# Max aggregation of a graph layer: which edge blocks are gathered and which are built by one-hot products, where the neighbour sums stand, and how the expert weights are fed

## The chip, the cores and the metric

The kernel runs on one core of a Trainium2 chip (trn2), as one launch. The metric is the time of one execution in device microseconds (us). The engines are named as in the profile: PE is TensorE, DVE is VectorE, ACT is ScalarE, POOL is GpSimd and SP is SyncE; PEld is PE's weight load. SP, ACT and POOL each issue DMAs into a queue of their own, and all queues are served by the core's 16 DMA engines.

## The reference

A graph transformer of two layers over N = 625 nodes of width 256 with E = 20,625 edges, sorted by destination. The second half of layer 0 and all of layer 1 matter here:

```python
x = x + L0_ffn(layernorm(x))                 # 8 experts, top 2 of each node
xn = layernorm(x)
msg = (xn @ W_bases)[src]                    # 128 numbers for each edge
agg_sym = segment_sum(msg * sym_w, dst)      # dense products with the adjacency matrix
agg_sum = segment_sum(msg, dst)
agg_max = segment_max(msg, dst)              # the largest of each node's incoming messages
h = einsum(weightings, [agg_sym, agg_sum, agg_max])
x = x + relu(graphnorm(h)) + lambda_attention(xn)
x = x + L1_ffn(layernorm(x))                 # 64 experts of 256 x 512 x 256, top 2 of each node
```

All numbers are float32. The 64 experts' weights alone are 67 MB.

## The kernel before, in words

**Tiling.** The nodes are 5 tiles (NT) of 125 (TP). The edges are 41 blocks (NMB) of 512 (MB); the last, block 40, has 145. Each engine has one program, written in order; semaphores join them. Nothing reorders instructions: what stands first on an engine or a queue goes first.

**End of layer 0.** POOL's `fetch(fys)` (L674) gathers each node's two expert rows into `ya` and `yb`, ten indirect DMAs of 125 rows. DVE's `add_results(0)` (L2168) adds them to `x`. SP issues the first two pairs of layer 1's expert weights (four DMAs of 1 MB, L585 and L586) before that. At the same time PE counts the edges of each node (L1170, 50 small matmuls), and DVE works out from them where each node's edges end (L2198 to L2207); on DVE that stands ahead of `add_results`.

**Bases and sums.** Then come the layer norm, the products with `W_bases` and `W_comb` (L1193, L1198), a store of the bases to DRAM as `btab` (ACT, L1570), a split of the bases into three bfloat16 parts (DVE, L2226 to L2232), and the neighbour sums: for each node tile 5 products of 125 x 256 with the adjacency matrix on PE (L1206) and two copies on DVE (L2240, L2242).

**The loop for the maximum.** For each block of edges the messages, 128 x 512, are brought into PSUM in one of two ways. An even block is built by 15 bfloat16 matmuls (3 parts x 5 node tiles, L1271) from a one-hot matrix, which DVE made for two such blocks at a time by comparing source numbers with node numbers (L2189, five instructions). An odd block is fetched by POOL from `btab` with four indirect DMAs of 128 rows (L729) and transposed by PE (four matmuls, L1277). There are four buffers for fetched blocks, and POOL waits for a buffer until PE has transposed the block that lay in it. DVE then runs a segmented running maximum over the block (L2389); PE transposes the result (L1287), ACT copies it out of PSUM, SP stores it to `rtab`. PE's order is: messages of block b, then the transposed runs of block b-2. The attention of the layer is strewn into the loop by block number: on PE queries (L819, after block 3), keys (L819), values (L1231), transposes (L1240), lambda (L1248), result (L1258); on DVE their counterparts, and from block 23 on the eight `weigh` steps of the sums (L1640, two instructions of 125 x 1280 each). After the loop POOL fetches each node's last run (L736), and DVE weighs the maxima.

**Layer 1's experts.** 32 steps of two experts each (64 node slots for each expert). Step s needs its rows, gathered by POOL (L670, four buffers), and its weights `W1` (1 MB, on SP's queue, L628) and `W2` (1 MB, on POOL's queue, L751). The weights lie in a ring of five pairs of SBUF regions (`EW_AT`, `RING`). Two pairs are loaded early, three more when the weighted sums are done (`c_out` 17, L620), the rest as steps free their regions: `W1` of step s when the hidden products of step s-5 are done, `W2` when the result products of step s-5 are done. PE's step is: transposed hidden rows of s-1 (L1391), transposed rows of s+1 (L1371), hidden products (L1382), result of s-1 (L1405). ACT stores each step's 128 result rows to `ys`.

**The end.** POOL waits for all stores, fetches two rows for each node (`ya` for five tiles, then `yb` for five), DVE adds all of `ya`, then all of `yb`, tests whether an expert was overfull, and SP stores the output as one DMA of 625 KB (L636).

## Time and profile before

| | us |
|---|---|
| median of 3 runs | 991.87 |
| lowest and highest run | 987.62, 994.85 |
| profiled execution | 991.11 |
| its span, first to last instruction | 989.4 |

The profile is of one execution. Its page gives busy time by engine; the chain of waits follows the work that ended last back from the end; the groups by line give the mean duration of each kind of instruction and what ended the idle time before it; the timeline gives instructions in order of time; the table by stretches gives busy time, granted TensorE clock and DMA load between two moments. Times in the rows are us from the start of the span. A busy PE is not PE at its peak, since ends of matmuls are modelled.

| part of the span | from, to (us) |
|---|---|
| layer 0's rows fetched and added | 478.8 to 507.2 |
| layer norm, bases, split, neighbour sums | 507.2 to 542.9 |
| loop for the maximum, to the last running maximum | 547.6 to 702.9 |
| last runs, weighing, graph norm, routing of layer 1 | 702.9 to 778.1 |
| 32 expert steps | 778.1 to 957.2 |
| fetch of results, output | 957.2 to 989.4 |

### The profile page before, as it was taken

What the parts mean: (1) busy time and instruction counts of PE and PEld (TensorE: products, weight loads), DVE (VectorE), ACT (ScalarE), POOL (GpSimd) and SP (SyncE); (2) the same over time, 40 slices, a digit from 0 to 9 for tenths busy, and PEclk for the clock granted to TensorE, in tenths of its full rate; (3) what the DMA queues carried; (4) which work ended last, traced back from release to release, by engine and by line L of the source; (5) the groups of instructions that cost most, each with busy time, mean ns of one, the idle gap of its engine ahead of it and who ended that gap; (6) DMA issues with size and microseconds to landing.
All of it is one profiled execution on the core that took longest, in us unless ns stands there. A gap on an engine that the chain in (4) does not pass through costs nothing.

```text
span 989.4 us, 13447 instructions
## 1 busy us (share of the span) xinstructions
PE 711.3 (72%) x4912; PEld 522.4 (53%) x4912; DVE 485.5 (49%) x1173; ACT 161.1 (16%) x355; POOL 198.0 (20%) x213
## 2 busy tenths in 40 slices
PE   2467767989979619999747789787333597878880
PEld 1355646877868519999545456444212244444440
DVE  7537888656663451111343265588686522222231
ACT  0311311224201104233000021111100011111110
POOL 3000000000000011231503545372200332232213
PEclk9978977899989759999658999898855699999995
DMA  3440100000000066998631355465251499999922
GB/s 110 91 135 1 50 1 1 1 2 1 2 1 2 9 203 215 326 321 277 181 109 37 98 135 155 110 181 141 82 219 62 128 381 410 410 410 410 410 84 72
DMA packets 84500, 147.75 MB, mean 149 GB/s; under 512 B 10961, under 2 KB 57641, under 8 KB 84428
## 3 DMA queue, kind: packets, MB, share of 16 engines
q1 hardware_dynamic: 58438, 84.97, 25.5%
q0 software_dynamic: 18336, 55.09, 16.5%
q10 hardware_dynamic: 7654, 6.75, 2.0%
q8 instruction: 43, 0.70, 0.3%
q14 instruction: 29, 0.24, 0.1%
HBM read 127.45 MB, written 19.31 MB: 148 GB/s over the span
## 4 chain that ended last, share of the span: by engine, by line
PE 48%; DVE 21%; DMA 14%; issue 4%; POOL 3%; ACT 1%; DVEq 1%; POOLq 0%; SPq 0%; ACTq 0%
DMA big<-xn_rows,spots 11%; PE ps L1271 6%; PE ps L1127 5%; PE ps L1141 5%; PE ps L932 5%; DVE arena L1640 4%; PE ps L819 3%; PE ps L978 3%; PE ps L1382 3%; PE ps L1405 2%; DVE arena L2389 2%; PE ps L943 2%; PE ps L918 2%; DVE big L1916 2%; DVE ya L1640 2%
## 5 line engine op out<-in xcount | busy, mean ns | idle before, releaser
L670 POOL DMA_INDIRECT big<-xn_rows,spots x46 | 45.1, 981 | 432.4 <-DVE spots L2047 409.1
L978 PE MATMUL ps<-big 125*128 125x144 bf16 x825 | 94.7, 242 | 19.8 <-DVE big L1640 11.6
L1640 DVE TENSOR_TENSOR arena<-arena,ps 125x400 f32 x110 | 57.9, 526 | 90.4 <-PE ps L980 80.2
L978 PEld LDWEIGHTS ps<-big 125*128 125x128 bf16 x825 | 84.5, 107 | 25.8 <-DVE big L1640 14.4
L1271 PE MATMUL ps<-arena,early 125*128 125x512 bf16 (+1 forms) x315 | 77.2, 402 | 21.7 <-DVE arena L2389 16.3
L980 PE MATMUL ps<-big 125*128 125x64 bf16 x825 | 92.6, 205 | 0.0
L980 PEld LDWEIGHTS ps<-big 125*128 125x128 bf16 x825 | 81.9, 104 | 6.7 <-issue 4.3
L1640 DVE TENSOR_TENSOR big<-ps,b1cols 128x512 f32<-128x512 f32 x32 | 22.1, 691 | 116.9 <-PE ps L1391 116.9
L2389 DVE TENSOR_TENSOR_SCAN arena<-arena,ps 128x512 f32<-128x512 bf16 (+1 forms) x41 | 51.6, 1257 | 47.5 <-PE ps L1287 36.1
L1271 PEld LDWEIGHTS ps<-arena,early 125*128 125x128 bf16 x315 | 31.1, 104 | 62.6 <-DVE arena L2389 19.6
L1382 PE MATMUL ps<-arena,big 128*64 128x512 f32 x256 | 63.7, 619 | 0.0
L1405 PE MATMUL ps<-arena,big 128*64 128x256 f32 x512 | 60.7, 379 | 1.3 <-issue 1.3
L1916 DVE TENSOR_SCALAR big<-iota,srcf 125x640 bf16<-125x640 f16 x165 | 57.9, 380 | 0.0
L932 PE MATMUL ps<-arena,xn 125*128 125x250 f32 (+1 forms) x240 | 51.0, 362 | 8.0 <-ACT tmpf L1476 6.7
L1127 PE MATMUL ps<-big,arena 128*128 128x128 f32 x448 | 54.3, 281 | 2.3 <-DVE big L2137 2.3
L1127 PEld LDWEIGHTS ps<-big,arena 128*128 128x128 f32 x448 | 53.9, 198 | 3.5 <-issue 2.9
L1405 PEld LDWEIGHTS ps<-arena,big 128*64 128x64 f32 x512 | 36.9, 137 | 32.8 <-issue 19.1
L729 POOL DMA_INDIRECT lwo<-btab,srcs x40 | 39.6, 990 | 67.2 <-issue 47.7
L1485 ACT COPY picks<-big 125x624 bf16<-125x624 bf16 x55 | 37.9, 707 | 84.6 <-DVE big L1640 84.2
L1141 PE MATMUL ps<-arena,big 128*128 128x256 f32 x224 | 50.7, 380 | 0.0
L932 PEld LDWEIGHTS ps<-arena,xn 125*128 125x128 f32 x240 | 41.3, 200 | 14.0 <-ACT tmpf L1476 8.1
L729 POOL DMA_INDIRECT kphi<-btab,srcs x40 | 41.2, 1030 | 34.3 <-PE ps L1277 23.6
(356 smaller groups left out, 1108.0 us busy)
## 6 DMA issues: line engine op xcount, KB each, us to landing
arena<-in_L_ffn_W_dram SPq DMA_DIRECT2D x53, 1024.0 KB, 10.2
arena<-in_L_ffn_W_dram POOLq DMA_DIRECT2D x39, 1024.0 KB, 16.5
rtab<-arena SPq DMA_DIRECT2D x40, 256.0 KB, 3.9
arena<-new_node SPq DMA_DIRECT2D x40, 128.0 KB, 3.3
ys<-big ACTq DMA_DIRECT2D x32, 128.0 KB, 7.3
arena<-src_list SPq DMA_DIRECT2D x20, 125.0 KB
arena<-in_L_mix_W_dram SPq DMA_DIRECT2D x2, 1024.0 KB, 6.9
fys<-big ACTq DMA_DIRECT2D x14, 128.0 KB, 3.1
```

Of the source, the lines that this page charges most:

```text
L729: pool.indirect_dma_start(fetched[i % 2][:, 4 * h + j, :], None, btab.ap(), bass.IndirectOffsetOnAxis(ap=srcs[:, c:c + 1].bitcast(U32), ax ...
L932: m = pe.matmul(ps[:, 6, 0:(t1 - t0) * TP], xn[:, s, c * 128:(c + 1) * 128], adj5[:, b, s, t0 * TP:t1 * TP], start=(s == 0), stop=(s == NT ...
L978: pe.matmul(psflat[:, at:at + K2 * WIN], ohs[:, s, u, t * TP:t * TP + 128], pieces[:, 0:K2 * WIN], start=first and t % 2 == 0, stop=False, ...
L980: m = pe.matmul(psflat[:, at + K1 * WIN:at + K2 * WIN], ohs[:, s, u, t * TP:t * TP + 128], pieces[:, K2 * WIN:KC * WIN], start=False, stop ...
L1127: m = pe.matmul(ps[:, 2 + 2 * (c % 2) + h, m_ * 128:(m_ + 1) * 128], fw1[:, c % 2, k, (4 * h + m_) * 128:(4 * h + m_ + 1) * 128], fxT[:, c ...
L1141: m = pe.matmul(ps[:, 6 + c % 2, 0:D], fh[:, c % 2, k, :], fw2[:, c % 2, k, :], start=(k == 0), stop=(k == 7))
L1271: m = pe.matmul(ps[:, 6 + b % 2, 0:n], split[:, t, k, :], onehot[:, i % 2, t, h * MB:h * MB + n], start=(k == 0 and t == 0), stop=(k == 2 ...
L1382: m = pe.matmul(ps[64 * e:64 * e + 64, 2 + s % 2, :], xeT[:, s % 2, k, 64 * e:64 * e + 64], ew[s % RING][0][:, e, k * H1:(k + 1) * H1], st ...
L1405: m = pe.matmul(ps[64 * e:64 * e + 64, 6 + s % 2, 0:D], hact[:, s % 2, k, 64 * e:64 * e + 64], ew[s % RING][1][:, e, k * D:(k + 1) * D], s ...
L1640: return v.tensor_tensor(out, p, q, op)
L1916: return v.tensor_scalar(ohs[:, s, u, :], iota16[0:EP, :], col, None, ALU.is_equal)
L2389: v.tensor_tensor_scan(runs[:, b % 2, 0:n], arep[:, b % 4, 0:n], ps[:, 6 + b % 2, 0:n], runs[:, (b - 1) % 2, MB - 1:MB] if b else -3e38, A ...
```

## The change

1. **Blocks.** Every third block (0, 3, ..., 39) and block 40 are built by one-hot products, 15 in all; the other 26 are fetched. Before it was 21 and 20. POOL issues 104 gathers in the loop in place of 80; DVE makes 8 one-hot sets in place of 11. There are still four buffers for fetched blocks.
2. **Neighbour sums.** They move into the loop: tiles 0 and 1 after block 0, tiles 2, 3, 4 after blocks 1, 2, 3, on PE and on DVE. The queries move from block 3 to 4 on PE and from 4 to 5 on DVE. PE tests for unsorted edges once in place of twice.
3. **`btab`** is stored by node tiles, five DMAs on ACT's queue.
4. **Weights behind the fetch.** SP waits for both halves of the fetch of layer 0's rows before it issues the first two pairs of expert weights.
5. **Ring of seven.** Two more pairs of regions, made of memory that is free by then (bias rows, the mixing weights, turned rows, old keys); buffers are merged so that they are contiguous. Five pairs are issued at `c_out` 17, but for the last `W2`, which waits for the routing (`spots_out` 2). The store of the normalised rows moves from SP to ACT.
6. **Results by tiles.** The last fetch goes tile by tile (`ya`, `yb` of tile 0, then tile 1, ...), DVE adds tile by tile, and SP stores each tile (125 KB) when it is added, without waiting for DVE's test.
7. Some semaphores are shared, to make room for others (`types_ready`, `comp_ready` and `row_ready` become counts of `edges_ready`); what waits for what is the same.

On PE, between the products with `W_bases` (L1193, now L1210) and the test that opens the loop. Before:

```order
L1193 MATMUL ps<-wbc,xnT 125x224 x10
L1198 MATMUL ps<-xnT,wbc 128x313 x4
L1206 MATMUL ps<-yb,arena 125x256 x25
L1291 TENSOR_LOAD loose
L1291 ISA x2
L1292 COMPARE_AND_BRANCH
```

And of the change, on PE at the same place:

```order
L1210 MATMUL ps<-wbc,xnT 125x224 x10
L1215 MATMUL ps<-xnT,wbc 128x313 x4
L1307 TENSOR_LOAD loose
L1307 ISA x2
L1309 COMPARE_AND_BRANCH
```

The 25 products of the neighbour sums (`yb,arena`) have left the place ahead of the test.

On PE, the first blocks of the loop. `arena,early` (now `arena,kept`) are the one-hot products, `ident,lwo` and `ident,kphi` (now `mixw`, `kept`) the transposes of a fetched block, `ident,arena` those of the runs. Before:

```order
L1271 MATMUL ps<-arena,early 128x512 x15
L1277 MATMUL ps<-ident,lwo 128x128 x4
L1271 MATMUL ps<-arena,early 128x512 x15
L1287 MATMUL ps<-ident,arena 128x128 x4
L1277 MATMUL ps<-ident,lwo 128x128 x4
L1287 MATMUL ps<-ident,arena 128x128 x4
L819 MATMUL ps<-xnT,wq 128x313 x8
```

And of the change, on PE, blocks 0 to 3:

```order
L1286 MATMUL ps<-arena,kept 128x512 x15
L1221 MATMUL ps<-yb,arena 125x256 x10
L1293 MATMUL ps<-ident,mixw 128x128 x4
L1221 MATMUL ps<-yb,arena 125x256 x5
L1293 MATMUL ps<-ident,mixw 128x128 x4
L1303 MATMUL ps<-ident,arena 128x128 x4
L1221 MATMUL ps<-yb,arena 125x256 x5
L1286 MATMUL ps<-arena,kept 128x512 x15
L1303 MATMUL ps<-ident,arena 128x128 x4
L1221 MATMUL ps<-yb,arena 125x256 x5
```

Two fetched blocks now stand in a row between one-hot blocks, and each of the first four blocks is followed by neighbour sums.

On POOL, the start of the expert steps: `big<-xn_rows,spots` is a gather of rows, `arena<-in_L_ffn_W_dram` the load of a `W2`. Before:

```order
L670 DMA big<-xn_rows,spots 128x256 [waits spots_out,xn_stored]
L670 DMA big<-xn_rows,spots 128x256 x3
L670 DMA big<-xn_rows,spots 128x256 [waits s_xT] x2
L751 DMA arena<-in_L_ffn_W_dram 128x2x1024 [waits s_y]
L670 DMA big<-xn_rows,spots 128x256 [waits s_xT]
L751 DMA arena<-in_L_ffn_W_dram 128x2x1024 [waits s_y]
```

And of the change, on POOL at the same place:

```order
L685 DMA big<-xn_rows,spots 128x256 [waits spots_out,xn_stored]
L685 DMA big<-xn_rows,spots 128x256 x3
L685 DMA big<-xn_rows,spots 128x256 [waits s_xT] x4
L764 DMA arena<-in_L_ffn_W_dram 128x2x1024 [waits s_y]
L685 DMA big<-xn_rows,spots 128x256 [waits s_xT]
L764 DMA arena<-in_L_ffn_W_dram 128x2x1024 [waits s_y]
```

The first `W2` that POOL loads stands behind two more gathers, and is that of step 7 in place of step 5.

The core of the diff:

```diff
-NSET = -(-NMB // 4)
-NGOT = NMB // 4
+SPREAD = [b for b in range(NMB) if b % 3 == 0 or b == NMB - 1]
+GOT = [b for b in range(NMB) if b not in SPREAD]
+NSET = -(-len(SPREAD) // 2)
...
-        RING = len(EW_AT)
+        ew.append([rows[:, 0:8, :].rearrange("p (e a) d -> p e (a d)", e=2),
+                   mixw[:, 0:2048].rearrange("p (e n) -> p e n", e=2)])
+        ew.append([turned2[:, 0:2048].rearrange("p (e n) -> p e n", e=2),
+                   kept2[:, 0:2048].rearrange("p (e n) -> p e n", e=2)])
+        RING = len(ew)
...
+            for k in range(2):
+                sp.wait_ge(y_got[k], 80)
             for s in range(2):
                 sp.dma_start(ew[s][0], w1v[s]).then_inc(ew1_loaded[s], 16)
                 sp.dma_start(ew[s][1], w2v[s]).then_inc(ew2_loaded[s], 16)
...
             sp.wait_ge(c_out, 17)
             for s in range(2, RING):
                 sp.dma_start(ew[s][0], w1v[s]).then_inc(ew1_loaded[s], 16)
-                sp.dma_start(ew[s][1], w2v[s]).then_inc(ew2_loaded[s], 16)
-            sp.wait_ge(norm_ready, 6)
-            sp.dma_start(node_major(xn_rows[1].ap()), xn[:, :, :]).then_inc(xn_stored, 16)
+                if s < RING - 1:
+                    sp.dma_start(ew[s][1], w2v[s]).then_inc(ew2_loaded[s], 16)
+            sp.wait_ge(xn_stored, 32)
+            sp.wait_ge(spots_out, 2)
+            sp.dma_start(ew[RING - 1][1], w2v[RING - 1]).then_inc(ew2_loaded[RING - 1], 16)
             for s in range(RING, E1 // 2):
                 sp.wait_ge(s_h, s - RING + 1)
                 sp.dma_start(ew[s % RING][0], w1v[s]).then_inc(ew1_loaded[s % RING], 16)
...
+                for t in range(NT):
+                    sp.wait_ge(sparse_done, t + 1)
+                    sp.dma_start(a["out"][t * TP:(t + 1) * TP, :], x[:, t, :]).then_inc(o_stored, 16)
+                sp.wait_ge(o_stored, 16 * NT)
...
-                for i in range(NGOT):
-                    for h in range(2):
-                        if i >= 2:
-                            pool.wait_ge(msg_mm, 4 * (i - 2) + 2 * h + 2)
-                        for j in range(4):
-                            c = 4 * (4 * i + 2 * h + 1) + j
-                            pool.indirect_dma_start(fetched[i % 2][:, 4 * h + j, :], None, btab.ap(),
...
+                for q, b in enumerate(GOT):
+                    if q >= 4:
+                        pool.wait_ge(msg_mm, GOT[q - 4] + 1)
+                    for j in range(4):
+                        c = 4 * b + j
+                        pool.indirect_dma_start(fetched[q // 2 % 2][:, 4 * (q % 2) + j, :], None, btab.ap(),
...
-            fetch(ys)
+            for t in range(NT):
+                for k in range(2):
+                    pool.indirect_dma_start((ya, yb)[k][:, t, :], None, ys.ap(),
...
-            pe.wait_ge(c_out, 7)
-            for t in range(NT):
-                if t >= 2:
-                    pe.wait_ge(c_out, 7 + t - 1)
+            def neighbour_sums(t):
+                pe.wait_ge(c_out, 7 if t < 2 else 7 + t - 1)
                 for s in range(NT):
                     m = pe.matmul(ps[0:TP, t % 2, 0:2 * DB], adjT[:, s, t * TP:(t + 1) * TP], bas[:, s, :],
                                   start=(s == 0), stop=(s == NT - 1))
                 cproduct(m)
-            pe.wait_ge(c_out, 12)
...
-                    if b == 3:
+                    if b == 0:
+                        neighbour_sums(0)
+                        neighbour_sums(1)
+                    if 1 <= b < NT - 1:
+                        neighbour_sums(b + 1)
+                    if b == 4:
                         attend_queries()
...
-            act.wait_ge(c_out, 5)
-            act.dma_start(node_major(btab.ap()), bas[:, :, 0:DB]).then_inc(btab_stored, 16)
+            for t in range(NT):
+                act.wait_ge(c_out, t + 1)
+                act.dma_start(btab.ap()[t * TP:(t + 1) * TP, :], bas[:, t, 0:DB]).then_inc(btab_stored, 16)
...
-            add_results(1).then_inc(sparse_done, 1)
-            dve.wait_ge(sparse_done, 1)
+            for t in range(NT):
+                dve.wait_ge(y_tile[t][0], y_tile[t][1] + 32)
+                done(v.scalar_tensor_tensor(out=x[:, t, :], in0=ya[:, t, :], scalar=gate[:, t, 2:3], in1=x[:, t, :],
+                                            op0=ALU.mult, op1=ALU.add))
+                v.scalar_tensor_tensor(out=x[:, t, :], in0=yb[:, t, :], scalar=gate[:, t, 3:4], in1=x[:, t, :],
+                                       op0=ALU.mult, op1=ALU.add).then_inc(sparse_done, 1)
+            dve.wait_ge(sparse_done, NT)
```

## Rows read from the trace of the kernel before

**Rows 1.** By stretches: us; busy PE, PEld, DVE, ACT, POOL; granted clock, DMA share, GB/s.

```profile
547.50:595.30 47.80, 42.56 (x201) 26.20 (x202) 23.44 (x33) 7.69 (x14) 22.26 (x24) 0.93 0.46 116
595.30:640.50 45.20, 37.91 (x194) 24.51 (x193) 26.96 (x46) 7.71 (x14) 19.73 (x21) 0.92 0.52 142
640.50:703.00 62.50, 49.09 (x267) 27.60 (x266) 54.17 (x56) 11.80 (x21) 26.75 (x24) 0.92 0.53 147
```

**Rows 2.** Timeline, end of layer 0: start, us, engine, instruction, idle before it.

```profile
487.86 10.66 PE L1170 MATMUL ps<-ones,arena 125*125 125x1 f32 x50 [0.51 <-DVE x L1640]
...
505.10 2.07 DVE L2173 SCALAR_TENSOR_TENSOR x<-yb,gate,x 125x256 f32<-125x256 f32 x5 [0.57 <-DMA yb<-fys,get]
```

**Rows 3.** Chain of waits, the fetch: start, us, what.

```profile
493.21 11.79 DMA yb<-fys,get
```

**Rows 4.** Timeline, from the bases to the first gather of the loop.

```profile
521.82 2.27 PE L1198 MATMUL ps<-xnT,wbc 128*128 128x313 f32 x8
...
527.02 0.82 DVE L1640 TENSOR_TENSOR early<-big,early 125x640 bf16<-125x640 f32 x1
...
529.00 13.25 PE L1206 MATMUL ps<-yb,arena 125*125 125x256 f32 x50 [4.91 <-DVE yb L2233]
531.78 0.96 POOL L729 DMA_INDIRECT lwo<-btab,srcs  x1 [37.37 <-issue]
```

**Rows 5.** Timeline of PE in the loop.

```profile
547.58 4.85 PE L1271 MATMUL ps<-arena,early 125*128 125x512 bf16 x15 [5.32 <-issue]
...
665.70 3.41 PE L1271 MATMUL ps<-arena,early 125*128 125x512 bf16 x15 [0.70 <-DVE arena L2389]
...
673.08 5.10 PE L1271 MATMUL ps<-arena,early 125*128 125x512 bf16 x15 [2.65 <-DVE arena L2389]
678.01 0.60 PE L1287 MATMUL ps<-ident,arena 128*128 128x128 f32 x4
```

**Rows 6.** Timeline of DVE in the loop: a one-hot set, a weigh step, block 40.

```profile
665.56 2.05 DVE L2189 TENSOR_SCALAR arena<-arena,nodeid 125x1024 bf16<-125x1024 f16 x5
...
670.22 1.49 DVE L1640 TENSOR_TENSOR ya<-ya,arena 125x1280 f32<-125x1280 f32 x1
...
702.41 0.52 DVE L2389 TENSOR_TENSOR_SCAN arena<-arena,ps 128x145 f32<-128x145 bf16 x1 [0.41 <-PE ps L1287]
```

**Rows 7.** Groups of POOL from 531 to 640: count, busy us, mean ns, idle before.

```profile
L729 POOL DMA_INDIRECT lwo<-btab,srcs x32 | 30.5, 954 | 64.7 <-issue 45.3 <-PE ps L1277 19.4
```

**Rows 8.** Groups of POOL from 640 to 680.

```profile
L729 POOL DMA_INDIRECT kphi<-btab,srcs x16 | 18.0, 1125 | 17.4 <-PE ps L1277 13.1 <-issue 4.3
```

**Rows 9.** Timeline of POOL, the slowest gather.

```profile
668.89 2.11 POOL L729 DMA_INDIRECT kphi<-btab,srcs  x1 [0.30 <-issue]
```

**Rows 10.** The gathers of the loop (L729) by themselves.

```profile
DMA to landing us min/median/max: 2.4/3.4/8.3
```

**Rows 11.** Table by stretches, as rows 1: ahead of the expert steps, and in them.

```profile
730.00:780.00 50.00, 15.43 (x62) 11.60 (x64) 35.29 (x115) 2.12 (x4) 4.73 (x5) 0.53 0.36 139
...
800.00:940.00 140.00, 116.12 (x737) 61.07 (x734) 36.80 (x72) 23.58 (x50) 40.27 (x47) 1.00 1.03 411
```

**Rows 12.** Timeline, first refills of the ring, SP's and POOL's.

```profile
782.88 26.77 SPq L628 DMA_DIRECT2D arena<-in_L_ffn_W_dram  x7
...
788.41 0.75 POOL L751 DMA_DIRECT2D arena<-in_L_ffn_W_dram  x1 [6.87 <-PE ps L1405]
```

**Rows 13.** Chain of waits, a step that waits for its rows, and the end.

```profile
918.35 17.43 DMA big<-xn_rows,spots
...
974.07 4.11 DMA yb<-ys,get
978.27 2.08 DVE x L2173 x5
```

**Rows 14.** Timeline, the output.

```profile
981.68 0.35 SPq L636 DMA_DIRECT2D out_dram<-x  x1
```

**Rows 15.** The stores of the steps' rows (L1615) by themselves.

```profile
DMA to landing us min/median/max: 1.7/7.3/9.4
```

More of the change, by code:

```diff
@@ L1291, in _ @@
             slow = pe.value_load(loose[0:1, 0:1], min_val=0, max_val=E)
+            products = nc_[0]
             with pe.If(slow > 0):
+                for t in range(NT):
+                    neighbour_sums(t)
                 attend_queries()
@@ L1328, in _ @@
             with pe.Else():
+                nc_[0] = products
                 pe.wait_ge(split_ready, 1)
@@ L2236, in _, with neighbour_sums @@
             m.then_inc(c_out, 1)
-            for t in range(NT):
+            def neighbour_sums(t):
                 dve.wait_ge(c_mm, 7 + t)
@@ L2335, in _ @@
             with dve.If(slow > 0):
+                for t in range(NT):
+                    neighbour_sums(t)
+                dve.wait_ge(c_out, 12)
                 weigh(0, 8)
@@ L2368, in _ @@
                 dve.wait_ge(mx_turned, 1)
-                for t in range(NT - 2):
-                    mark_free(v.memset(held[:, :], 0.0))
                 mark_free(v.tensor_copy(agg[:, 0:4, 2 * DB:3 * DB],
```

135 lines of the change are left out of this document (73 added, 62 removed).

## The prediction

> **What bounds the kernel now.** I read the chain of waits first, then the stretches, then the timeline of each engine around the six edits. Three stretches matter.
>
> The loop for the maximum runs from PE's first one-hot product at 547.58 [rows 5] to DVE's last running maximum at 702.41 + 0.52 = 702.93 [rows 6], 155.4 us. No single engine fills it. In its first part (blocks 0 to 9) PE is busy 42.6 of 47.8 us, in the second (10 to 20) 37.9 of 45.2, in the third (21 to 40) DVE 54.2 of 62.5 [rows 1]. POOL is busy less than half of each. The rest is PE and DVE waiting for one another.
>
> The expert steps are held by DMA: from 800 to 940 its share is 1.03 at 411 GB/s [rows 11], and a step waits for its rows, which land 17.43 after their issue behind the weights [rows 13]. Ahead of the steps, from 730 to 780, DMA is busy only 0.36.
>
> The fetch at the end of layer 0 looks like a third: its last gather takes 11.79 to land [rows 3], beside 4 MB of weights, against 4.11 for the same gather in the end [rows 13]. But DVE's addition of `yb` had idled only 0.57 for it [rows 2].
>
> **The change, part by part.**
>
> *Weights behind the fetch.* Without the weights the last gather lands about 493.2 + 4.1 = 497.3, eight earlier. PE's 50 counting products (487.86 to 498.52 [rows 2]) and what DVE makes of them stand ahead of the additions, and are not touched. So only the 0.57 goes; from then on the counts are what is late. The weights move behind the fetch, about 497 to 508, where they hide under the layer norm; the loop's lists are ahead of them on SP's queue. Term: **-0.6**, carried into the loop's start.
>
> *Neighbour sums and the test.* PE is free of the bases at 521.82 + 2.27 = 524.1; the split is ready at 527.84 [rows 4]. The two tests ahead of the loop cost 5.32 of idle PE [rows 5]; one costs between half of that and all, so PE is through between 526.8 and 529.4. I take 528.4, the middle and later than the split, less the 0.6: the first one-hot product at **527.8** in place of 547.58.
>
> *`btab` by tiles, start of the gathers.* The first gather is at 531.78 [rows 4]. Five stores in place of one may end a microsecond earlier or later; I take nothing but the 0.6: **531.2**.
>
> *The loop, by PE and DVE.* A one-hot block costs PE 3.41, or 5.10 after an idle time of 2.65; a fetched one 0.60 [rows 5], so each exchange saves PE 2.8. First part: PE's 42.6, plus the sums' 13.25 [rows 4], less 2.8 for one exchange (five one-hot blocks become four) is 53.0; at the higher clock the sums are some 2 shorter, waits are 0 to 2: I take 52. Second part: 37.9 less three exchanges is 29.5, plus the 7.3 that PE idles now is 36.8; since block 21's one-hot now stands behind the attention's result I take 38. Third part: DVE's 54.2 less one set of one-hots (2.05 [rows 6]) is 52.1, and of its 8.3 idle, which were mostly waits for one-hot blocks, I keep 3: 55. Together 145, so the last maximum would be at 527.8 + 145 = 672.8.
>
> *The loop, by POOL.* It now has 26 blocks of four gathers. A gather takes 0.954 + 0.30 [rows 7, 9] while DVE is little used, 1.125 + 0.30 beside the weigh steps [rows 8, 9]. With 72 of the first and 32 of the second kind, 90.3 + 45.6, the last is issued by 667.1 if the four buffers never hold POOL up, and lands 3.4 later [rows 10], at 670.5. Block 38 is the last fetched; after it come its transposes, two one-hot blocks (one short), their turns and maxima, about 7.5 by rows 5 and 6: 678. That is the later of the two sums and they are close, so each will now and then wait for the other: I take **679**. Term: 702.9 - 679 = **-24**. Ends: 670 if they interleave without loss (-33), 690 below. The early move of the queries by a block and the shared semaphores cost nothing: PE does the work of block 4 meanwhile, and the counts rise in the old order.
>
> *Ring of seven.* Four megabyte DMAs leave the saturated stretch: 4.19 MB at 411 GB/s is 10.2 us. They go to the stretch from 730, where 139 of some 410 GB/s are used [rows 11]; five pairs are there by about 23 us after their issue, before the steps begin. Against it: POOL's first `W2` stands behind two more gathers, each freed by a turned block, and comes about 1.7 later than now (788.41 [rows 12]), which at half the bandwidth is 0.9; and `W1` (released from 782.88 on) can run further ahead of rows and `W2` than now, which leaves PE more steps to do after the last byte. For that I take 1.3. Term: **-8**; ends -14 (DMA and PE end together) and 0. The last `W2` goes out beside the first rows and may hold up the first step: **+0.5** (0 to 1.5). The rows' store on ACT's queue is hidden by the routing, which lasts to 774.
>
> *Results by tiles.* The ten gathers end as now. DVE then has two of ten instructions left, 0.83 in place of 2.08 [rows 13], and SP needn't wait for DVE's test: it issues at about 979.1 in place of 981.68 [rows 14], 2.6 earlier. From there to the span's end (989.4) 7.7 pass now for 625 KB. For 125 KB the store may take as little as 1.7 [rows 15], or, if the time is all fixed, 7.7; I take 4.8. Term: **-5.5**; ends -2.6 and -8.6.
>
> A page of the Trainium skill speaks against that term. "DMA: Bandwidth & Descriptors", section "Anatomy of one DMA", gives a DMA about 2.0 us plus its bytes at 436 GB/s; by it the shorter store would save only 1.2 and the term would be -3.8. The 7.7 above holds more than it states, so the trace does not settle it.
>
> **Sum.** -24 - 8 + 0.5 - 5.5 = -37. The profiled execution took 991.1, so 954.1; the median of the runs is 0.8 above it, so **955**.
>
> **The rivals.**
>
> *The gathers set the pace throughout.* POOL's idle times for a free buffer go, and DVE is denser than now, so all 104 may take 1.425: 148.2. Then the last maximum is at 531.2 + 148.2 + 3.4 + 7.5 = 690.3 and the loop gives 12.6: 966. For it: rows 8 against rows 7. Against it: in the first two parts DVE has no weigh steps. Chance 0.2.
>
> *All overlaps work.* PE and DVE interleave (-33), the ring gives 12, the end 8: -52.5, so 939. For it: PE's 13 us of sums fall into waits for the first gathers. Against it: the three engines hand over for each block. Chance 0.14.
>
> *The ring gives nothing.* Steps wait for rows, not for weights [rows 13]; if the rows queue longer behind more weights, PE ends where it does now: 963. Against it: DMA is saturated, and it has 10 us less to move. Chance 0.08.
>
> *DVE shuts POOL out.* If POOL waited out each of DVE's one-hot sets (six in the loop, 2.05 each) and weigh steps (sixteen of about 1.49 [rows 6]), 36 us, the gathers would need 104 x 1.254 + 36 = 166.4, the loop would end at 708.5, 5.6 later than now: 984. Rows 8 show 0.17 a gather beside such work, not a whole instruction, and one of 2.11 [rows 9]. Chance 0.05.
>
> The Trainium skill, "SBUF — State Buffer", section "Who interferes with whom", states such a rule: VectorE in a two-port mode holds the port pair that GpSimd needs to write descriptors for the whole instruction. By it the gathers would be about as in the last paragraph; the trace shows the effect, at a tenth of that size.
>
> *Slower: gathers crowd each other out.* 26 blocks' gathers run beside the same stores and lists in a shorter loop. Each gather would have to take over 1.67 for the kernel to lose what ring and end give (531.2 + 104 x 1.67 + 10.9 = 715.8, which is +13), and 1.77 for 1% more. At 1.9 the loop ends at 739.7: 1016. For it: the 2.11 + 0.30 of the slowest gather [rows 9]. Against it: DMA's share in the loop is about half [rows 1]. Chance 0.03.
>
> **How the numbers follow.** The forecast, 948 to 962, has 0.5. Below 940 lies about half of the second rival (0.07), above 970 the last two (0.08); so 940 to 970 holds a little over 8 in 10. About 1%, some 10 us, is what a measurement of this kernel can tell from no change, its three runs being 7 apart. Faster by more than that: all cases but the last two, 0.92; within it: the shut-out POOL, 0.05; slower: 0.03.
>
> **What would show it.** The addition of `yb` waits for nothing, and DVE's count is what precedes it. The first one-hot product stands near 528 and the neighbour sums lie among the first blocks. POOL waits for few buffers, and its gathers step by 1.25, later 1.4; the last maximum is near 679. Seven pairs are loaded by 775 on the old clock, and DMA is saturated some 10 us less. The last output store is issued within a microsecond of the last addition. It is wrong if the gathers step by over 1.5, if the loop takes more than 160 us from its first product, or if the steps' total stays at 179 us.

## The result, and the profile after

The changed kernel takes **954.31 us** (median of 4 runs, 950.98 to 958.77) against 991.38 for the kernel before beside it: a ratio of **0.963**, 95% interval 0.958 to 0.968. Forecast were 955 in a range of 940 to 970. The time fits; not all of its terms do, and one stretch of the profiled execution owes nothing to the change.

The profiled execution took 950.98, the fastest of the four; its span is 949.3 against 989.4. The stretches of the loop, cut as in [rows 1] (us; busy PE, PEld, DVE, ACT, POOL; granted clock, DMA share, GB/s):

```profile
521.70:575.70 54.00, 47.95 (x229) 33.25 (x230) 25.59 (x43) 7.64 (x14) 38.40 (x41) 0.94 0.45 119
575.70:614.90 39.20, 33.54 (x186) 23.60 (x184) 24.91 (x41) 7.81 (x14) 29.93 (x31) 0.96 0.66 176
614.90:676.00 61.10, 44.29 (x233) 24.89 (x232) 52.52 (x51) 11.57 (x20) 36.32 (x33) 0.86 0.57 156
```

They took 54.0, 39.2 and 61.1 us; forecast were 52, 38 and 55. POOL is now busy for two thirds of the loop. The third stretch is where the forecast is off: the granted clock is 0.86 there, and DVE, busy 52.5 of 61.1, waits for one-hot products.

The timeline (start, us, engine, line, instruction, number, and in brackets the idle time before it and what ended it). L1187 are PE's counting products, L2199 the additions of layer 0's rows, L1286 the one-hot products, L743 the gathers, L2416 the running maximum, L1404 the first hidden product of a step, L651 the output:

```profile
474.59 0.70 PE L1079 MATMUL ps<-ident,picks 125*8 125x125 f32 x5 [1.67 <-issue]
...
480.90 10.66 PE L1187 MATMUL ps<-ones,arena 125*125 125x1 f32 x50 [0.51 <-DVE x L1666]
...
497.97 2.07 DVE L2199 SCALAR_TENSOR_TENSOR x<-yb,gate,x 125x256 f32<-125x256 f32 x5
...
515.63 2.27 PE L1215 MATMUL ps<-xnT,wbc 128*128 128x313 f32 x8
...
521.70 4.99 PE L1286 MATMUL ps<-arena,kept 125*128 125x512 bf16 x15 [3.81 <-DVE kept L1666]
...
525.06 0.96 POOL L743 DMA_INDIRECT mixw<-btab,srcs  x1 [32.70 <-issue]
...
626.70 5.10 PE L1286 MATMUL ps<-arena,kept 125*128 125x512 bf16 x15 [2.28 <-DVE arena L2416]
...
638.00 4.87 PE L1286 MATMUL ps<-arena,kept 125*128 125x512 bf16 x15 [3.14 <-DVE arena L2416]
...
659.20 6.20 PE L1286 MATMUL ps<-arena,kept 125*128 125x512 bf16 x15 [3.13 <-DVE arena L2416]
...
675.40 0.52 DVE L2416 TENSOR_TENSOR_SCAN arena<-arena,ps 128x145 f32<-128x145 bf16 x1 [0.41 <-PE ps L1303]
...
752.54 3.68 PE L1404 MATMUL ps<-arena,big 128*64 128x512 f32 x8 [0.25 <-DVE big L2503]
...
756.26 9.99 SPq L640 DMA_DIRECT2D arena<-in_L_ffn_W_dram  x3
...
765.20 0.77 POOL L764 DMA_DIRECT2D arena<-in_L_ffn_W_dram  x1
...
933.99 12.56 SPq L651 DMA_DIRECT2D out_dram<-x  x5
...
945.77 0.48 DVE L2526 SCALAR_TENSOR_TENSOR x<-yb,gate,x 125x256 f32<-125x256 f32 x1
```

Against [rows 2]: `yb` is added with no wait, where it had waited 0.57. Against [rows 4, 5]: the first one-hot product stands at 521.70, 6.1 behind the start of L1215; before, 25.8 lay between the same two. Against [rows 6]: the last maximum ends at 675.92. Against [rows 12]: the refills begin at 756.26 (SP) and 765.20 (POOL), 3.7 and 12.7 behind the first hidden product, where they had come 3.7 and 9.2 behind it. Against [rows 14]: the last output store is issued at 946.3, right behind the last addition (945.77 + 0.48), and the span ends 3.0 later; from the store to the end it had been 7.7.

The gathers by themselves (for [rows 7 to 10]), with what they waited for and who waited for them:

```profile
L743 POOL DMA_INDIRECT mixw<-btab,srcs x56: 940/947/1718, 525.1 to 660.2; - x56
...
  PE ps L1293: 1.0, 3
...
  PE ps L1293: 2.9, 2
...
DMA to landing us min/median/max: 2.4/3.5/6.7
```

POOL makes 104 gathers (these 56 and 48 into the other buffer, `kept`) from 525.06 to 661.16, one each 1.309 us; buffers held it up for 1.0 us in all, and PE waited for gathered rows for 2.9. Four waits of the expert steps remain in the chain of waits, for [rows 13]:

```profile
800.36 20.94 DMA big<-xn_rows,spots
822.12 23.90 DMA big<-xn_rows,spots
846.85 24.06 DMA big<-xn_rows,spots
871.74 22.09 DMA big<-xn_rows,spots
```

The chain of the kernel before has six such waits, of 16.3 to 19.2; now there are four, of 21 to 24.

### The profile page after: what moved, and what is told of

The parts are those of the page before. It is cut to its first block, busy times and chain, and to the rows that moved or that the text cites. A ratio compares the mean times of both kernels' runs of the same rounds, so it can differ in the third digit from the quotient of the medians.

```text
span 949.3 us, 13321 instructions
## 1 busy us (share of the span) xinstructions
PE 692.8 (73%) x4846; PEld 514.7 (54%) x4846; DVE 480.1 (51%) x1158; ACT 161.2 (17%) x355; POOL 220.8 (23%) x235
## 4 chain that ended last, share of the span: by engine, by line
PE 51%; DVE 21%; DMA 13%; issue 3%; POOL 2%; ACT 1%; DVEq 1%; POOLq 0%; ACTq 0%; SPq 0%
DMA big<-xn_rows,spots 11%; PE ps L1144 6%; PE ps L1158 5%; PE ps L949 5%; PE ps L1286 4%; DVE arena L1666 4%; PE ps L836 4%; PE ps L1404 3%; PE ps L995 3%; PE ps L1427 3%; DVE arena L2416 2%; PE ps L960 2%; PE ps L935 2%; DVE big L1942 2%; DVE ya L1666 2%
## 5 line engine op out<-in xcount | busy, mean ns | idle before, releaser
L995 PE MATMUL ps<-big 125*128 125x144 bf16 x825 | 94.3, 241 | 19.2 <-DVE big L1666 11.5
L1286 PE MATMUL ps<-arena,kept 125*128 125x512 bf16 (+1 forms) x225 | 57.9, 418 | 19.9 <-DVE arena L2416 16.1
L2416 DVE TENSOR_TENSOR_SCAN arena<-arena,ps 128x512 f32<-128x512 bf16 (+1 forms) x41 | 51.5, 1257 | 39.3 <-PE ps L1303 32.9
L743 POOL DMA_INDIRECT mixw<-btab,srcs x56 | 55.8, 997 | 49.5 <-issue 49.2
L743 POOL DMA_INDIRECT kept<-btab,srcs x48 | 48.8, 1018 | 14.7 <-issue 14.0
L1286 PEld LDWEIGHTS ps<-arena,kept 125*128 125x128 bf16 x225 | 22.8, 108 | 51.5 <-DVE arena L2416 18.7
L1404 PE MATMUL ps<-arena,big 128*64 128x512 f32 x192 | 50.4, 648 | 0.2 <-DVE big L2503 0.2
L1427 PE MATMUL ps<-arena,big 128*64 128x256 f32 x384 | 46.2, 383 | 1.3 <-issue 1.3
L1158 PEld LDWEIGHTS ps<-arena,big 128*128 128x128 f32 x224 | 41.5, 190 | 5.1
## 6 DMA issues: line engine op xcount, KB each, us to landing
turned<-in_L_ffn_W_dram SPq DMA_DIRECT2D x4, 1024.0 KB, 16.6
```

Source lines behind the costliest of these rows:

```text
L743: pool.indirect_dma_start(fetched[q // 2 % 2][:, 4 * (q % 2) + j, :], None, btab.ap(), bass.IndirectOffsetOnAxis(ap=srcs[:, c:c + 1].bitca ...
L995: pe.matmul(psflat[:, at:at + K2 * WIN], ohs[:, s, u, t * TP:t * TP + 128], pieces[:, 0:K2 * WIN], start=first and t % 2 == 0, stop=False, ...
L1158: m = pe.matmul(ps[:, 6 + c % 2, 0:D], fh[:, c % 2, k, :], fw2[:, c % 2, k, :], start=(k == 0), stop=(k == 7))
L1286: m = pe.matmul(ps[:, 6 + b % 2, 0:n], split[:, t, k, :], onehot[:, i % 2, t, h * MB:h * MB + n], start=(k == 0 and t == 0), stop=(k == 2 ...
L1404: m = pe.matmul(ps[64 * e:64 * e + 64, 2 + s % 2, :], xeT[:, s % 2, k, 64 * e:64 * e + 64], ew[s % RING][0][:, e, k * H1:(k + 1) * H1], st ...
L1427: m = pe.matmul(ps[64 * e:64 * e + 64, 6 + s % 2, 0:D], hact[:, s % 2, k, 64 * e:64 * e + 64], ew[s % RING][1][:, e, k * D:(k + 1) * D], s ...
```

## The experiments

Each is the changed kernel with the edit shown (the last three with several), timed beside the kernel before on the same chip, which took 989.1 to 989.6 us each time. "The control" is the first of them, and +x us is the difference of the medians to it. The stretches below are from one profile each; the medians judge.

### The changed kernel again

> The changed kernel itself, unaltered, as the yardstick for the others of this call. Both theories: 954 us, ratio 0.963 to the kernel before (0.958 to 0.968). Its one profile is looked at for the idle time of TensorE ahead of the counting products of layer 0, which was 5.69 us in the kernel before and 1.67 us in the changed one: if that gap belongs to the changed program, it is again 1.5 to 2 us; if it varies from execution to execution, it may be 5 to 6.

955.21 us (949.23 to 957.81), ratio 0.964 (0.961 to 0.968). Its profile, of 955.88, shows ahead of layer 0's expert bias:

```profile
479.32 1.20 PE L1079 MATMUL ps<-ident,picks 125*8 125x125 f32 x5 [5.92 <-issue]
```

The same program that idled 1.67 there now idles 5.92. Among 14 profiles (before, after, and the twelve here) the gap is 1.67 or 1.68 in three and 4.89 to 6.50 in eleven, the kernel before among these. The counting products stand at 486.66 here, so 5.8 of the 7.0 us that those of the profile above are earlier (487.86 to 480.90) are of that execution, not of the change; 4.25 of them are this gap. This second profile is the fairer partner of the one before:

| stretch, us | before | changed (c0) | difference | forecast |
|---|---|---|---|---|
| start to the counting products | 487.9 | 486.7 | -1.2 | 0 |
| to the first one-hot product | 59.7 | 39.7 | -20.0 | -19.8 |
| the loop, to the last maximum | 155.4 | 154.5 | -0.9 | -4.1 |
| to the first hidden product | 76.3 | 77.3 | +1.1 | |
| the expert steps | 178.0 | 171.3 | -6.7 | -7.5 |
| behind the last result product | 32.3 | 24.7 | -7.5 | -5.5 |
| span | 989.4 | 954.2 | -35.2 | -37 |

The table says when things happen, not which edit pays for it: the neighbour sums left the second row and entered the third. That is what the undoing is for.

### Weights ahead of the fetch again

```diff
-            for k in range(2):
-                sp.wait_ge(y_got[k], 80)
             for s in range(2):
                 sp.dma_start(ew[s][0], w1v[s])...
```

> The first four loads of expert weights of layer 1 (two W1, two W2) go out at once again, ahead of the fetch of layer 0's rows, as in the kernel before; all else is the changed kernel. Theory (the fetch had been late for DVE by 0.57 us only, so nearly all of it was hidden): 955 us, 0.5 to 0.7 us more than the changed kernel, and DVE waits 0.4 to 0.7 us ahead of its add of the yb rows. Rival (the loads also held up TensorE, and the 4 us that its counting products start earlier after the change come from here): 958 to 960 us, and in its profile TensorE idles 5 to 6 us ahead of the counting products.

957.48 us (956.84 to 959.67), ratio 0.967 (0.964 to 0.971): 2.3 above the control, with overlapping intervals. Its addition of `yb`:

```profile
504.89 2.07 DVE L2197 SCALAR_TENSOR_TENSOR x<-yb,gate,x 125x256 f32<-125x256 f32 x5 [1.15 <-DMA yb<-fys,get]
```

A wait of 1.15 in place of none, and PE's gap is 6.16, no longer than the control's 5.92. The order of the weights is worth one to two microseconds, a little more than the theory's 0.7; the rival's 4 us aren't from it.

### Ring of five

```diff
+        ew = ew[:5]
         RING = len(ew)
...
-                if s < RING - 1:
-                    sp.dma_start(ew[s][1], w2v[s]).then_inc(ew2_loaded[s], 16)
-            sp.wait_ge(xn_stored, 32)
-            sp.wait_ge(spots_out, 2)
-            sp.dma_start(ew[RING - 1][1], w2v[RING - 1]).then_inc(ew2_loaded[RING - 1], 16)
+                sp.dma_start(ew[s][1], w2v[s]).then_inc(ew2_loaded[s], 16)
```

> Ring of five weight sets in place of seven, with all nine or ten halves loaded as the kernel before did (both halves of sets 2 to 4 behind the sum over the nodes); all else is the changed kernel. Theory (the stretch of the expert steps is paced by weight bytes once the ring is used up, and two more sets were worth 6.2 us of it net, forecast 7.5): 960 to 962 us, the stretch from the first hidden product to the last result product 177 to 179 us in place of 171.7. Rival (two sets more give nothing, the 6 us are from elsewhere): 953 to 955 us and 171 to 173.

963.72 us (957.81 to 964.84), ratio 0.972 (0.969 to 0.976): +8.5. The expert steps take 179.9 from the first hidden to the last result product (756.96 to 936.81), against 171.3 in the control; the loop takes 153.9 (154.5 there). The rival falls; the ring is worth a little more than the theory's 6.2.

### One output store

```diff
-                for t in range(NT):
-                    sp.wait_ge(sparse_done, t + 1)
-                    sp.dma_start(a["out"][t * TP:(t + 1) * TP, :], x[:, t, :]).then_inc(o_stored, 16)
-                sp.wait_ge(o_stored, 16 * NT)
+                sp.wait_ge(sparse_done, NT)
+                sp.dma_start(node_major(a["out"]), x[:, :, :]).then_inc(o_stored, 16)
+                sp.wait_ge(o_stored, 16)
```

> The result is stored by one transfer behind the last tile's sum, as in the kernel before, not by five tile by tile; the fetch and the sums stay tile by tile. Theory (from the last sum to the end of the span it took 9.0 us before, 3.1 us after; the store was worth most of the end's 7.2 us): 958 to 960 us, and 7.5 to 9 us from the last sum to the end of the span. Rival (the five stores hide no more than one does, and the gain at the end came from sums made while rows were still being fetched): 954 to 955 us.

960.84 us (958.31 to 965.08), ratio 0.971 (0.967 to 0.974): +5.6. In the timeline:

```profile
953.08 0.48 DVE L2525 SCALAR_TENSOR_TENSOR x<-yb,gate,x 125x256 f32<-125x256 f32 x1
953.59 0.35 SPq L650 DMA_DIRECT2D out_dram<-x  x1
```

From the issue of the whole store to the end of the span (961.9) pass 8.3 us; from that of the last fifth 3.0. That is the gain of the end but for about 2 us: two additions stand behind the last rows in place of five, and SP no longer waits for DVE's test (in the kernel before the store was issued 1.3 us behind the last addition, here at once).

### Sums ahead of the loop

```diff
                 nc_[0] = products
+                for t in range(NT):
+                    neighbour_sums(t)
                 pe.wait_ge(split_ready, 1)
...
-                    if b == 0:
-                        neighbour_sums(0)
-                        neighbour_sums(1)
-                    if 1 <= b < NT - 1:
-                        neighbour_sums(b + 1)
```

(and the same on DVE)

> The neighbour sums are made ahead of the loop on TensorE and VectorE again, as in the kernel before, but with the loop's one test; all else is the changed kernel. Theory (inside the loop they cost TensorE 11.4 us of products in a first stretch where it is busy for 48 of 54 us, so moving them in gave only a part of the 13 to 14 us that they take ahead of it): 959 us (957 to 963), first one-hot product 13 to 14 us later, loop 5 to 11 us shorter. Rival (inside the loop they fill time in which TensorE waits and cost nothing): 967 to 969 us and a loop as long as the changed kernel's 154.

955.21 us (953.41 to 956.36), ratio 0.965 (0.964 to 0.967): the control's time to the last digit. Neither theory gave zero. PE of this kernel, then of the control, from the sums (L1221) to the queries' products (L836):

```profile
528.75 13.39 PE L1221 MATMUL ps<-yb,arena 125*125 125x256 f32 x50 [4.91 <-DVE yb L2256]
541.98 3.40 PE L1286 MATMUL ps<-arena,kept 125*128 125x512 bf16 x15
...
552.68 4.38 PE L836 MATMUL ps<-xnT,mixw 128*128 128x313 f32 x16
```

```profile
526.40 6.25 PE L1286 MATMUL ps<-arena,kept 125*128 125x512 bf16 x15 [3.81 <-DVE kept L1666]
532.48 4.48 PE L1221 MATMUL ps<-yb,arena 125*125 125x256 f32 x20
...
550.96 4.45 PE L836 MATMUL ps<-xnT,mixw 128*128 128x313 f32 x16
```

With the sums ahead, the first one-hot product is 15.6 later, but the queries come 1.7 later only, and L1215 had begun 1.3 later already. PE is busy nearly without a gap in either order, so moving its own work does nothing: what came off ahead of the loop was put into it. Even the wait for the split (3.81, now ahead of the one-hot product) has its twin (4.91, ahead of the sums), and the first one-hot product takes 3.40 behind 13.4 us of products, but 6.25 behind an idle time. From L1215 to the first one-hot product it is 20.4 here and was 25.8 in the kernel before: the **tests** give about 5.3. The branches of PE's sequencer (PEldq; ns, then when they begin), of the kernel before and, below, of the changed one:

```profile
L1292 PEldq COMPARE_BRANCH  x1: 339/339/339, 543.5 to 543.5; - x1
L1302 PEldq COMPARE_BRANCH  x1: 2840/2840/2840, 544.6 to 544.6; - x1
```

```profile
L1309 PEldq COMPARE_BRANCH  x1: 3545/3545/3545, 515.0 to 515.0; - x1
```

The gain is the place of the test, not that there is one less. The branch that is left takes longer than both before, but it stands ahead of a wait of PE and is over at 518.6, when PE still waits for the split until 521.7 (with the sums ahead: 3.28, over at 524.7, while PE waits for the bases until 528.75). In the kernel before both tests stood behind the sums, where PE waited for nothing else. And the loop without the sums takes 140.3 against 155.4 before: the **exchange of blocks** gives some 15.

### Half the blocks by one-hot products, a quarter

```diff
-SPREAD = [b for b in range(NMB) if b % 3 == 0 or b == NMB - 1]
+SPREAD = [b for b in range(NMB) if b % 2 == 0]
```

> Every second edge block by one-hot products (21 of 41 in place of 15), the other 20 by 80 gathers in place of 104, as in the kernel before; sums in the loop, ring and end as changed. Theory (the exchange of blocks pays: six blocks more cost TensorE about 5.0 against 1.2 us each, and VectorE three sets of 2.05 us): loop 164 to 170 us, 965 to 970 us in all. Rival (the loop fell from 155.4 to 154 although the sums went in, so the exchange gave little; something else paces it): 953 to 957 us.

968.97 us (967.44 to 969.53), ratio 0.979 (0.978 to 0.981): +13.8; the loop takes 165.2 (522.61 to 687.80). The exchange pays as expected; POOL, with 80 gathers, waited 34.5 us for buffers.

With `b % 4 == 0`:

> Every fourth edge block by one-hot products (11 of 41), 30 by 120 gathers; all else as changed. Theory (POOL's step of 1.309 us is next behind TensorE: 120 gathers take 157 us from 529.7, the last lands at 689 to 690, the loop ends 9 to 12 us later): 963 to 967 us, and TensorE waits for gathered rows in the last stretch. Rival (TensorE and VectorE set the pace, and four one-hot blocks fewer save them 15 us, half of it on the path): 946 to 950 us.

971.83 us (966.85 to 974.70), ratio 0.981 (0.979 to 0.983): +16.6, more than expected; the loop takes 170.8 (527.68 to 698.46). PE's waits for gathered rows (us in total, times, longest):

```profile
PE ps L1293 <- DMA mixw<-btab,srcs: 18.9, 7, 4.8
PE ps L1293 <- DMA kept<-btab,srcs: 16.2, 5, 5.0
```

35 us of waiting, against 1.4 in the control: here POOL is the bound. Of the three shares tried a third is the best; both neighbours cost 14 to 17 us.

### Four PSUM banks

```diff
-                    pe.wait_ge(run_step, b - 1)
+                    pe.wait_ge(run_step, b - 1 if b < 22 else b - 3)
...
+def bank(b):
+    return 6 + b % 2 if b < 22 else (6, 7, 0, 1)[b % 4]
```

(the blocks' products, transposes and maxima use `bank(b)` in place of `6 + b % 2`)

> From block 22 on the messages of the blocks take four PSUM banks in turn in place of two (the two others are free by then), so that TensorE may begin a block's products one running maximum earlier; all else as changed. Theory (in the last third of the loop VectorE waits some 8 us for one-hot products that could start only when the running maximum two blocks back was done; with the bank free they start while VectorE still weighs): the stretch from 614.9 to 676.0, 61.1 us, takes 54 to 57, 948 to 951 us in all. Rival (the waits belong to VectorE's own work and to the low clock, and move elsewhere): 953 to 956 us.

953.85 us (946.69 to 955.99), ratio 0.962 (0.959 to 0.965): not apart from the control. The timeline of the last third:

```profile
641.26 4.35 PE L1292 MATMUL ps<-arena,kept 125*128 125x512 bf16 x15
...
649.93 1.03 PE L1299 MATMUL ps<-ident,mixw 128*128 128x128 f32 x4 [3.00 <-DMA mixw<-btab,srcs]
...
660.89 1.09 PE L1299 MATMUL ps<-ident,kept 128*128 128x128 f32 x4 [2.64 <-DMA kept<-btab,srcs]
...
672.09 1.08 PE L1299 MATMUL ps<-ident,mixw 128*128 128x128 f32 x4 [4.24 <-DMA mixw<-btab,srcs]
...
673.82 5.13 PE L1292 MATMUL ps<-arena,kept 125*128 125x512 bf16 x15
...
679.60 1.93 DVE L2422 TENSOR_TENSOR_SCAN arena<-arena,ps 128x512 f32<-128x512 bf16 x2 [4.05 <-PE ps L1309]
```

The one-hot products do begin without a wait. In their place PE waits 3.00, 2.64 and 4.24 for gathered rows. The wait was taken away, and POOL, a few us behind, took its place: the stretch fell from 61.8 to 58.8 only. So two bounds of the loop lie near each other here.

### The pattern moved by a block

```diff
-SPREAD = [b for b in range(NMB) if b % 3 == 0 or b == NMB - 1]
+SPREAD = [b for b in range(NMB) if b % 3 == 1 or b == 0]
```

> The same numbers of blocks by one-hot products (15) and by gathers (26), but the pattern moved by one block: one-hot are 0, 1, 4, 7, ... 37, 40 in place of 0, 3, 6, ... 39, 40. All else as changed. Theory (at the loop's start TensorE waits for what the first eight gathers bring, whether the sums stand ahead of the loop or in it, since the gathers start at 530 either way and step by 1.3; and behind the last gather there are two one-hot blocks): the queries' products, at 551 in the changed kernel, stand at 545 to 549; from the last gather's issue to the last maximum it takes 10 to 12 us in place of 15; 948 to 952 us. Rival (TensorE's and VectorE's work alone sets the loop's length, whatever the order of the blocks): 954 to 956 us.

967.25 us (965.77 to 969.90), ratio 0.978 (0.976 to 0.980): **+12**, where both theories had at most +1. My theory of the loop's start falls: the queries stand at 551.72, no earlier. In the timeline, turns of runs (L1303) that wait for ACT:

```profile
574.82 1.09 PE L1303 MATMUL ps<-ident,arena 128*128 128x128 f32 x4 [5.19 <-ACT arena L1607]
...
612.33 1.09 PE L1303 MATMUL ps<-ident,arena 128*128 128x128 f32 x4 [4.44 <-ACT arena L1607]
...
614.92 6.27 PE L1286 MATMUL ps<-arena,kept 125*128 125x512 bf16 x15 [1.50 <-DVE arena L2416]
```

ACT copies a block's turned runs into one of two buffers, which come free when the store to `rtab` has landed (42 us of ACT's waits end with such a store). Here PE idles 5.19 and 4.44 behind such copies (once, 2.43, in the control), and after the second the next one-hot product takes 6.27. In the control ACT waits even longer for stores in all (53 us); what differs is that PE stands behind it twice. By the end of the attention's result this loop is 12.4 behind the control (627.7 against 615.4), 3.4 of it the one-hot block that now stands ahead and 7.2 PE's longer waits for ACT; from there on both need 65.5 or 65.6.

### The same pattern with banks and weigh steps eased

```diff
+WEIGH_AT = (4, 11, 15, 20, 24, 27, 30, 33)
...
-                    if b in range(23, 39, 2):
-                        weigh((b - 23) // 2, (b - 23) // 2 + 1)
+                    if b in WEIGH_AT:
+                        weigh(WEIGH_AT.index(b), WEIGH_AT.index(b) + 1)
```

(with the four banks and the moved pattern; a wait of DVE moves from block 5 to 4 with the first of these steps)

> As the shifted pattern, with four PSUM banks from block 22 on and the eight weigh steps behind blocks 4, 11, 15, 20, 24, 27, 30, 33 in place of 23, 25, ... 37. Theory (with banks alone TensorE waited 12.5 us for gathered rows, and VectorE's work fills the last third; with both eased POOL's 136 us are the bound): the last maximum 5 to 8 us behind the last gather's issue, so at 672 to 675 us against 681; 945 to 949 us. Rival (POOL is not the bound, and VectorE's steps only move): 950 us or more, with TensorE waiting under 3 us for gathered rows.

960.53 us (956.73 to 962.89), ratio 0.970 (0.968 to 0.972): 6.7 better than the moved pattern alone, 5 worse than the control. A miss, and not the rival's case either: PE waited 9.1 us for gathered rows. It waited for ACT once more, 14.6 us in six waits.

With 17 one-hot blocks and 24 gathered:

```diff
+SPREAD = [0, 1, 2, 4, 7, 10, 12, 15, 17, 20, 22, 25, 27, 30, 33, 36, 40]
```

> As the one before, with 17 blocks by one-hot products (0, 1, 2, 4, 7, 10, 12, 15, 17, 20, 22, 25, 27, 30, 33, 36, 40) and 24 by 96 gathers. Theory (POOL was the bound of the one before; eight gathers fewer free 10.5 us of it, and TensorE pays 3 to 5 us a block for two): 942 to 946 us, 3 us below the one before, with TensorE waiting under 4 us for gathered rows. Rival (TensorE is the bound by then): 4 to 8 us above the one before.

964.98 us (962.01 to 966.02), ratio 0.975 (0.973 to 0.977): 4.5 above the one before, the rival's size. PE waited 3.4 us for gathered rows and 13.3 for ACT. Fewer gathers didn't help here. That the loop is now held by its stores is the reading of these waits, not shown by a run: how much of these three runs' loss is the store and how much the order of the attention's steps, wasn't taken apart.

### Pattern of the changed kernel, banks, and the last block gathered

```diff
-SPREAD = [b for b in range(NMB) if b % 3 == 0 or b == NMB - 1]
+SPREAD = [b for b in range(NMB - 2) if b % 3 == 0] + [NMB - 3, NMB - 1]
...
-                    if b in range(23, 39, 2):
-                        weigh((b - 23) // 2, (b - 23) // 2 + 1)
+                    if b == 20 or b in range(23, 37, 2):
+                        weigh((b - 21) // 2 if b > 20 else 0, (b - 21) // 2 + 1 if b > 20 else 1)
```

(with the four banks)

> The pattern of the changed kernel, with four PSUM banks from block 22 on, block 38 by one-hot products and block 39 by gathers (so that only the short block 40 stands behind the last gathered one), and the weigh steps one place earlier (behind blocks 20, 23, 25, ... 35). Theory (with four banks TensorE waited 9.9 us for gathered rows at blocks 32, 35 and 38, and a one-hot product of 5.1 us stood behind the last of them; now it is made while those rows come): from the last gather's issue to the last maximum 7 to 9 us in place of 12.9, 947 to 951 us. Rival (the length of the loop hangs on how one-hot products and VectorE's steps fall on one another, as the pattern moved by one block showed, and any move here costs as much as it gives): 953 to 960 us.

**946.92 us** (943.27 to 951.54), ratio **0.959** (0.956 to 0.961): below both kernels. Its end of the loop:

```profile
660.86 3.40 PE L1292 MATMUL ps<-arena,kept 125*128 125x512 bf16 x15
...
666.13 0.63 PE L1299 MATMUL ps<-ident,mixw 128*128 128x128 f32 x4 [1.43 <-DMA mixw<-btab,srcs]
...
667.40 1.93 DVE L2422 TENSOR_TENSOR_SCAN arena<-arena,ps 128x512 f32<-128x512 bf16 x2 [1.22 <-PE ps L1309]
```

The one-hot product of block 38 is made while the last rows come, and from the issue of the last gather (662.1) to the last maximum (669.33) pass 7.2 us, as the theory had. The loop takes 149.0 against the control's 154.5; these 5.5 are of the three edits together. Its profile, of 943.27, has the short gap (1.68) ahead of the expert bias; the median is over five runs. Its interval just touches the control's, so that it is faster than the changed kernel is likely, not certain.

## Why the prediction was right, and where it wasn't

**Weights behind the fetch** (-0.6). Right: the wait of 0.57 is gone, and 1.15 comes back when the edit is undone. What seemed 7 us in the first profile is 1.2 in the second; no edit stands there.

**First one-hot product** (547.58 to 527.8). Right in size: 19.98 less between counting products and first one-hot product, forecast 19.8 with the fetch's 0.6. Its step for the test was wrong, and luck that this cost little: I let one test, at half of 5.32 or more, run behind the bases' products and end 0.6 behind the split (528.4 is also not the middle of 526.8 and 529.4, which is 528.1). The test ran beside these products and ended 3.1 ahead of the split, and the split alone set the time (the wait of 3.81 for `kept`). And the term isn't a gain for its larger part: the sums' 14 us go into the loop and stay there whole (undone: 0.0). What is left is the tests' 5.3.

**The loop by PE and DVE** (145). This step failed: 154.5. The third stretch was put at 55 and took 61 to 62. I kept 3 of 8.3 us of DVE's waits; it still waits 8.6 (61.1 less 52.5). Four of the products it waits for take 4.87 to 6.20, after idle times of 2.1 to 3.1, and can't start until the maximum two blocks back has left their bank: with four banks they start without a wait. The other two stretches are 2 and 1 longer than forecast. **The loop by POOL** (151, 679) was the later of the two sums and gave the answer: the last maximum is at 680.85. It was right by a bound that doesn't bind. The gathers themselves came as forecast, 136.1 us for 135.9; but from the last one's end to the last maximum 14.8 passed, forecast 10.9, and PE waits only 1.4 to 2.9 us for gathered rows, all at the loop's start. Only when the banks are eased does it (9.9 us), and by then nearly nothing is left to win. Two sums within 6 us of each other made the total safe, not the reasoning; and that the whole is right to 1 us is luck, since the loop gave 3 us less than forecast, the end 2 more and the start 1 more.

**Ring of seven** (-7.5 net). Right: 6.7 by the profiles, 8.5 by undoing it. The bytes left the stretch as forecast: 352 GB/s for 171.3 us in place of 363 for 178.0 are 4.3 MB less, and in the 48 us ahead DMA moves 215 GB/s in place of 140.

**Results by tiles** (-5.5). Too small: 7.5, of which the store is 5.4 to 5.6. I took the middle between 1.7 and 7.7 for the last store to the end of the span; it is 3.0, near the low end, while the whole one takes 8.3 (7.7 in the kernel before). The Trainium skill, "DMA: Bandwidth & Descriptors", section "Anatomy of one DMA", gives its 2.0 us plus bytes at 436 GB/s for DMAs that GpSimd issues, by which the difference would be an estimated 1.2. These stores go out on SP's queue, the runs show 5.3, and they decide.

**The rivals.** Gathers that set the pace throughout would need 1.425 each; they take 1.309. That DVE shuts POOL out falls by its price, not by its kind. The mean of [rows 8] hid that a gather does wait out DVE:

```profile
626.57 1.46 DVE L1666 TENSOR_TENSOR arena<-weights,big 125x1280 f32<-125x1280 f32 x1
...
627.13 1.72 POOL L743 DMA_INDIRECT mixw<-btab,srcs  x1 [0.30 <-issue]
```

This slowest gather ends 0.82 us behind the end of the weigh instruction in which it began (628.85 and 628.03). Twelve of the 104 begin in one, and all twelve end 0.81 to 0.82 behind its end; the 2.11 of [rows 9] is such a gather too. But each waits only for the rest of one instruction, and the median is 0.95: the twenty gathers of more than 1 us cost 6.3 us over it, where I had added up 36. The Trainium skill, "SBUF — State Buffer", section "Who interferes with whom", has DVE in a two-port mode hold the ports that it shares with GpSimd for its whole instruction, and has `tensor_tensor`, the weigh steps' kind, conflict only with what GpSimd reads. The trace agrees that a gather waits until such an instruction is over; for which port, no run here shows. All overlapping without loss wanted a loop of 142 (527.8 to 670); the nearest that a run with the sums in the loop came is the 149.0 of the last experiment. The ring did not give nothing, and the crowding gathers (1.67 each) did not come.

By undoing, then: blocks 13.8, ring 8.5, store 5.6, fetch 1 to 2, sums 0. With the tests' 5.3 and about 2 for the additions by tile and DVE's test at the end, both from profiles, that is 36 to 37; the change gave 37.1 in its first timing and 34.3 in the second.

## What to carry to other kernels

Before moving a busy engine's work from one place to another, ask which engine bounds the place where it lands: if it is the same one, the gain is only in the waits on either side. Look also at what the move leaves ahead of a wait, like the test here: it costs nothing while the engine waits for something else. In a loop that three engines share, compare the sums of all of them and of the stores behind them; when two lie within a few per cent, easing one shows the next, and the order in which kinds of blocks alternate can cost as much as their number. A mean hides who waits for whom: set the slowest instructions of one engine beside what the other engines ran at that moment. And take a second profile of the same program before crediting an edit with a stretch that it doesn't touch.

## What was not expected of the hardware

The gap of PE ahead of layer 0's expert bias is 1.7 us in 3 profiles and 4.9 to 6.5 in 11, with "issue" as its cause, in programs that don't differ there. It is one branch of PE's sequencer, in the first profile and in the control:

```profile
L464 PEldq COMPARE_BRANCH  x1: 431/431/431, 474.1 to 474.1; - x1
```

```profile
L464 PEldq COMPARE_BRANCH  x1: 4677/4677/4677, 474.6 to 474.6; - x1
```

In each of the three the profiled run is the fastest of its kernel, in none of the eleven. So the branch may be about half of the 9 us by which runs of one kernel differ; what makes it short was not found.

The last store of 125 KB is done 3.0 us after its issue, the whole 625 KB in one 8.3.

A one-hot block's 15 products (bf16, 512 columns) lose more to the clock than [rows 5] showed. The control by two short stretches, the first one-hot block, behind an idle time of 3.81, and the second, behind other products (columns as in the first table):

```profile
526.40:532.40 6.00, 6.00 (x15) 2.22 (x16) 1.04 (x5) 0.00 (x0) 2.06 (x3) 0.52 0.13 35
544.20:547.40 3.20, 3.20 (x16) 1.50 (x15) 0.55 (x2) 0.00 (x0) 2.29 (x4) 1.00 0.57 163
```

The first runs at a granted clock of 0.52, close to the lower level (1.2 GHz), and takes 6.25; the second at the full 2.4 GHz, and takes 3.40. The idle time alone doesn't fix the price: behind the same 3.81 the first block took 4.99 in the first profile. In the first profile's last third, PE idles 2.06 to 3.14 ahead of four such blocks, which take 4.87 to 6.20 where others take 3.41. With four banks the same four took 3.40 to 4.35; but the block after them, behind 4.24 of idle time, took 5.13 where it had taken 3.41.
